# Keys of a pair formed ahead of the leaf products of the pair in front; convolution and token activation run while the matrix is on its way through DRAM

## The chip, the cores and the metric

One core of a Trainium2 chip runs the whole program. TensorE (PE) does matrix products into eight PSUM banks, VectorE (DVE) and ScalarE (ACT) work elementwise, GpSimd (POOL) does copies, differences and indirect transfers, and SyncE (SP) issues most transfers. Each engine runs its instructions in program order and waits on semaphores for the others. The metric is the device time of one execution in microseconds (us).

## The reference

A layer on x of shape (16, 256, 128): a recurrent attention, LayerNorm, a feed-forward part over eight experts, LayerNorm. What matters here is the attention, for 8 heads with keys of 64 and values of 128 elements:

```python
h = _rms(x, w_norm_in)
conv = conv_b + sum((hp[:, j:j + T, :] * conv_w[:, j] for j in range(CK)))   # CK = 4, causal
h = jax.nn.silu(conv)
q, k, v = h @ wq, h @ wk, h @ wv                    # q and k are scaled to unit length per head
sd = h @ w_spike
ab = jax.nn.silu(h @ w_au + b_au) @ w_ad + b_ad     # the low-rank path
bb = h @ w_beta + b_beta
# for each time step t of 256:
mem = DECAY * mem + sd[t]; hard = mem > THR; mem = mem - hard * THR
s = s * alpha[..., None]                            # alpha from ab and the spikes
s = s + beta[..., None] * k[t] (v[t] - k[t] s)      # delta rule, shortened
out[t] = s^T q[t]
...
gate = sigmoid(silu(x @ w_u1 + b_u1) @ w_u2 + b_u2)
y = x + (y @ w_out) * gate
y = y + (silu(h2 @ w_ff1) * (h2 @ w_ff3)) @ w_ff2   # h2 = _rms(y, w_ffn)
```

## The kernel before, in words

The 256 time steps are cut into 8 chunks of 32 (`CH`); a chunk holds 32 steps of all 16 sequences, 512 tokens (`TOK`), and is worked on as a whole. `iterations` writes the body once for the first chunk, once in a hardware loop for chunks 1 to 6, and once for the last. `body(c, nxt, last)` is chunk c's work, into which the front of the next chunk (`nxt`: normalisation, convolution, membranes, decays) and the head of the chunk before (`last`: gate, feed-forward of the attention block, LayerNorm, routing) are woven. The order on each engine is that in which the code is written. A pass has three stages.

1. **The pairs.** The 8 heads go in 4 pairs p (`HP`). On PE `keys(c, p)` forms k and q of a pair from h (L1114, into the banks `read` and `write`). ACT's `keys` copies them to SBUF (L882), ACT's `squares` squares them out of the same banks (L891, into r and w) and so frees the banks; PE's `squares` sums these over the head by a matmul with an indicator (L1128) and so frees r and w for the next pair (`kqsq_used`). ACT's `factors` makes a pair's eight exponentials of decays (L921 to L931) from differences that GpSimd takes. DVE's `leaf_products(c, p)` multiplies keys and exponentials (L1521, L1522); PE's `leaves` forms the products within blocks of 8 steps (L1146). `cross_products` (L1532 to L1547) and PE's `crosses` (L1170, L1171) do the same between blocks; the last of these products is kend, which PE's `turn_ends` transposes (L1238). `turn` and `project` (L1219, L1228) finish the output of the chunk before, and `mean_square` (L1063) is the normalisation's mean for the next chunk. `mask_leaves`, `mask_cross` and `unit_rows_of` put a triangular matrix of 32 by 32 per head and sequence together; `norms` and `scaled_rows` (L1616) scale its rows.
2. **The solve.** SP stores the matrix to DRAM (`a_d`, L658) and loads it back, turned so that a partition holds one matrix (`na`, which lies in kq_blk, L664). DVE inverts it in `solve` by 31 steps j of two instructions (L1643, L1649), the second using the first's result. Between them stand instructions that do not depend on them: `membrane(n)`, 64 instructions (L1440, L1443) that run the next chunk's membranes through its 32 steps, each on the result of the one before, and the head's stages, which the table `stages` puts behind certain j. `pace` lets PE run the head's matmuls and two fillers (L1286) at every fourth j. `convolve(nxt)` (L1398 to L1405) stands in the stage before, at pair 2, behind `unit_rows_of`; `silus(nxt)` (L1416 to L1423) at the end of that stage: it makes h, waits for PE's low-rank matmul and makes au. ACT's `tokens` gives both their tanh. PE's `tokens` (L1071, L1076) forms the low-rank input and the drives sd0 to sd3, and ACT's `drives` copies these to mem (L852); DVE's `driven` waits for them.
3. **The tiles.** With the inverse (`u_d`, loaded to ub) eight tiles of 4 heads are read, predicted and written: r (L1719) is values less prediction; PE L1307, L1322, L1334, L1349; the state is L1729. `decays(nxt, step)` is woven in.

The head begins in the solve: PE multiplies x with wu1 (`u1`, L233), DVE makes zu (L330), ACT its tanh (`tu`, L293), DVE the product (L333); PE `u2`, ACT `gate` (L296), DVE `y1` (L337, L340), then `h2`, four feed-forward stages 0 to 3, and row statistics. Its x comes by a transfer that SP issues as the first thing of its pass, into the buffer that holds the normalisation's factor until the convolution has read it:

```python
            if last:
                sp_e.wait_ge(hn_ready.sem, hn_ready.at(nxt if nxt else c, 1))
                settle(c)
                sp_e.dma_start(xsq[:, :], a["xT"][last.loop + last.plus]).then_inc(hd.x_loaded.sem, 16)
            sp_e.wait_ge(ca_ready.sem, ca_ready.at(c, HP))
```

hn is the first result of `convolve`; ca is what `scaled_rows` writes.

## Time and profile before

| | us |
|---|---|
| median of 3 runs (lowest to highest) | 1876.25 (1864.84 to 1890.15) |
| the profiled execution | 1873.82 |
| its span in the profile | 1871.8 |
| busy: PE, DVE, ACT, POOL | 1449.1, 1274.1, 634.8, 360.1 |

The profile is of one execution. Its timeline lists the instructions of an engine in order of time; times count from the start of the span. Engines are not busy all the time, and no engine is the bound of the whole: which wait ends last has to be read from each stage. A busy PE is partly modelled, since matmuls overlap.

### The profile page before, as it was taken

How to read it: one execution, taken by the hardware profiler on the slowest of the kernel's cores; microseconds unless marked ns; L12 is line 12 of the kernel's file. 1: busy time of each engine (PE TensorE's matmuls, PEld its weight loads, DVE VectorE, ACT ScalarE, POOL GpSimd, SP SyncE). 2: the span in 40 equal slices, each digit the busy share in tenths (PEclk: the TensorE clock that was granted, in tenths of full speed). 3: DMA queues.
4: the chain of work that ended last, by engine and by line, in shares of the span. 5: the costliest groups of instructions: out<-in, count | busy, mean ns of one | idle time of the engine just before them, and what ended most of it. 6: DMA issues, size and time to landing. Idle time of an engine off the chain costs nothing. (4 is left out here: it accounts for less than half of the span.)

```text
span 1871.8 us, 46841 instructions
## 1 busy us (share of the span) xinstructions
PE 1449.1 (77%) x18540; PEld 946.9 (51%) x18568; DVE 1274.1 (68%) x3341; ACT 634.8 (34%) x1342; POOL 360.1 (19%) x515
## 2 busy tenths in 40 slices
PE   1687988797878887787879786888869897974685
PEld 0343664365525653465436562566436663652665
DVE  5568576966787667866796578765695678534564
ACT  4430243223422262134312352124312442222564
POOL 1210141014201320015101420023001420110232
PEclk8568996899689987998789979896699968996898
DMA  8980001010010001000100001000101000102223
GB/s 252 322 254 18 8 8 30 2 23 20 8 23 21 5 20 29 18 8 19 30 13 12 20 8 23 21 5 19 30 11 19 13 14 12 24 26 99 69 70 125
DMA packets 128139, 81.97 MB, mean 44 GB/s; under 512 B 75185, under 2 KB 118513, under 8 KB 127922
## 3 DMA queue, kind: packets, MB, share of 16 engines
q1 hardware_dynamic: 124466, 69.94, 13.6%
q0 software_dynamic: 3456, 8.95, 1.5%
q8 instruction: 159, 2.61, 0.6%
q14 instruction: 58, 0.48, 0.1%
HBM read 27.72 MB, written 51.15 MB: 42 GB/s over the span
## 5 line engine op out<-in xcount | busy, mean ns | idle before, releaser
L789 POOL COPY kx<-kend_t 32x256 f32<-32x256 f32 x256 | 114.3, 447 | 807.3 <-PE ps L1349 787.5
L1286 PE MATMUL ps<-wv,ident 128*128 128x512 f32 x320 | 173.7, 676 | 10.6 <-DVEq L1654 10.5
L1729 DVE SCALAR_TENSOR_TENSOR state<-state,gam,ps 128x128 f32<-128x128 f32 x512 | 137.4, 339 | 49.1 <-PE ps L1349 49.1
L1673 DVE TENSOR_TENSOR nv<-ps,nrm 128x512 f32<-128x512 f32 x64 | 44.2, 691 | 175.9 <-PE ps L1209 175.4
L1349 PE MATMUL ps<-w,kx 128*64 128x128 f32 x2048 | 127.1, 277 | 0.0
L1643 DVE TENSOR_TENSOR nv<-kq,kq_blk 128x31 f32<-128x31 f32 (+15 forms) x248 | 113.7, 458 | 16.7 <-ACT mem L852 10.8
L1349 PEld LDWEIGHTS ps<-w,kx 128*64 128x64 f32 x2048 | 111.7, 138 | 12.9 <-issue 12.9
L1521 DVE TENSOR_TENSOR kq_leaf<-kq,eleaf 128x1024 f32<-128x1024 f32 x32 | 39.9, 1247 | 112.6 <-ACT kq L882 112.4
L1286 PEld LDWEIGHTS ps<-wv,ident 128*128 128x128 f32 x320 | 66.7, 218 | 94.0 <-issue 77.5
L233 PE MATMUL ps<-eleaf,wf 128*128 128x512 f32 x112 | 62.0, 681 | 50.9 <-DVEq L1654 31.8
L999 ACT ACTIVATE w<-ps 128x512 f32<-128x512 f32 x64 | 38.2, 597 | 173.8 <-PE ps L1307 173.8
L1649 DVE TENSOR_TENSOR kq<-kq,nv 128x31 f32<-128x31 f32 (+15 forms) x248 | 91.5, 369 | 1.1
L1334 PE MATMUL ps<-state,kq_start 64*32 64x128 f32 x2048 | 82.9, 277 | 11.1
L1197 PE MATMUL ps<-state,kq_start 64*32 64x128 f32 x2048 | 82.1, 275 | 5.6
L1012 ACT ACTIVATE ysb<-ps 128x512 f32<-128x512 f32 x64 | 38.3, 598 | 141.6 <-PE ps L1334 141.6
L1228 PE MATMUL ps<-yt,wout 128*128 128x128 f32 x512 | 69.9, 293 | 20.0 <-ACT yt L898 20.0
L1307 PEld LDWEIGHTS ps<-r,ub 128*128 128x128 f32 x512 | 65.3, 194 | 36.2 <-issue 32.2
L1307 PE MATMUL ps<-r,ub 128*128 128x128 f32 x512 | 70.4, 281 | 14.2 <-DVE r L1719 11.8
L1170 PEld LDWEIGHTS ps<-kq_pair 64*32 64x32 f32 x2048 | 50.7, 122 | 58.0 <-issue 52.1
L1209 PE MATMUL ps<-wv,hv 128*128 128x512 f32 x128 | 78.3, 698 | 0.6 <-issue 0.2
L1228 PEld LDWEIGHTS ps<-yt,wout 128*128 128x128 f32 x512 | 64.0, 203 | 25.9 <-issue 19.0
L1322 PE MATMUL ps<-w,ab 32*32 32x128 f32 x2048 | 69.7, 273 | 6.0 <-ACT w L999 6.0
(313 smaller groups left out, 3303.9 us busy)
## 6 DMA issues: line engine op xcount, KB each, us to landing
slot_d<-row SPq DMA_DIRECT2D x16, 2064.0 KB, 20.3
xin<-slot_d SPq DMA_DIRECT2D x39, 129.0 KB, 2.1
a_d<-yt SPq DMA_DIRECT2D x8, 512.0 KB, 2.6
kq_blk<-a_d SPq DMA_DIRECT2D x32, 128.0 KB, 2.8
u_d<-kq SPq DMA_DIRECT2D x8, 512.0 KB, 2.6
ub<-u_d SPq DMA_DIRECT2D x128, 32.0 KB, 1.9
wall<-in_w SPq DMA_DIRECT2D x8, 512.0 KB, 7.9
xt<-in_xT POOLq DMA_DIRECT2D x8, 256.0 KB, 3.4
```

Of the source, the lines that this page charges most:

```text
L789: m = pool.tensor_copy(kx[part, :, b4, :], kend_t[part, g, 2 * q:2 * q + 2, :])
L1197: m = pe.matmul(bp.t[CH * b4:CH * b4 + CH, DV * hq:DV * hq + DV], kq_start[rows, hp, 0, CH * b:CH * b + CH], state[rows, hp, b, :], start= ...
L1209: pe.matmul(bv.t[:, :], hv[:, P * g:P * g + P], wv[:, 512 * q:512 * q + 512], start=True, stop=True).then_inc(bv.full.sem, 1)
L1228: m = pe.matmul(bp.t[:, 0:P], wout[:, hh, :], yt[:, hh, :], start=(hh == 0), stop=(hh == H - 1))
L1286: pe.matmul(bw.t[:, :], ident[:, :], wv[:, 0:512], start=True, stop=True)
L1307: m = pe.matmul(bw.t[:, DV * hq:DV * hq + DV], ub[:, g % 2, 4 * q + hq, :], r[:, hq, :], start=True, stop=True)
L1322: m = pe.matmul(by.t[part, cols], ab[part, hp, 1, 2 * g + h2, :], w[part, hq, :], start=(hq == 0), stop=False)
L1334: m = pe.matmul(by.t[CH * b4:CH * b4 + CH, cols], kq_start[rows, hp, 1, CH * b:CH * b + CH], state[rows, hp, b, :], start=False, stop=(hq ...
L1349: m = pe.matmul(bd[b4 % 2].t[DK * h2:DK * h2 + DK, o:o + DV], kx[:, j, b4, DK * h2:DK * h2 + DK], w[:, 2 * j + h2, :], start=True, stop=True)
L1643: dve.tensor_tensor(prod, tu[:, 0:n, j:j + 1].broadcast_to([P, n, m]), na[:, j + 1:CH, j].unsqueeze(1).broadcast_to([P, n, m]), ALU.mult). ...
L1649: i = dve.tensor_tensor(tu[:, 0:n, j + 1:CH], tu[:, 0:n, j + 1:CH], prod, ALU.subtract)
L1729: k = dve.scalar_tensor_tensor(out=state[:, hp, b, :], in0=state[:, hp, b, :], scalar=gam[:, hp, b:b + 1], in1=bd[j].t[:, DV * x:DV * x + ...
```

## The change

Five things are written in another order, and ScalarE gets one small instruction.

- PE: `keys(c, 1)` stands directly behind `keys(c, 0)`; for p from 1 on `keys(c, p + 1)` and `squares(c, p)` stand ahead of `leaves(c, p)`. Before, `leaves` came first, keys behind it and squares behind `crosses`.
- ACT: for pairs 2 and 3 keys, `ends_turned` and squares come first, `factors` behind them; `factors` came first before. `keys(c, 1)` stands ahead of `turned`.
- DVE: `convolve(nxt)` moves out of the pairs to the start of `solve`, behind the last `scaled_rows`; `silus` is split. The token part (h) stands between the head's zu and u1, the low-rank input (zau) behind step j = 0 and its product (au) behind j = 2.
- The membranes start at j = 6; they started at j = 0. The head's stages move to later j.
- ACT: a tanh of one column (`table_probe`) stands ahead of the wait for the convolution, and the low-rank tanh moves behind the head's `tu`.

```diff
@@ ScalarE
         def tokens(f):
 
+            act.activation(table_probe[:, :], eps_t[:, 0:1], ACT.Tanh)
             act.wait_ge(conv_step.sem, conv_step.at(f, 4))
...
             squares(c, 0)
             factors(c, 1)
+            keys(c, 1)
             if last:
                 turned(last, NG - 1)
-            keys(c, 1)
             squares(c, 1)
...
             for p in range(2, HP):
+                keys(c, p)
+                ends_turned(c, p - 2)
+                squares(c, p)
                 factors(c, p)
-                ends_turned(c, p - 2)
                 if nxt:
                     (square_x, rsqrt_x)[p - 2](nxt)
-                keys(c, p)
-                squares(c, p)
...
             if nxt:
+                low_rank(nxt)
                 drives(nxt)
@@ TensorE
             keys(c, 0)
+            keys(c, 1)
+            leaves(c, 0, runs)
             squares(c, 0)
-            leaves(c, 0, runs)
             if last:
                 turn(last, NG - 1)
-            keys(c, 1)
             crosses(c, 0, runs)
             if last:
                 project(last, NG - 1)
-            squares(c, 1)
             turn_ends(c, 0)
             for p in range(1, HP):
-                leaves(c, p, runs)
                 if p + 1 < HP:
                     keys(c, p + 1)
+                squares(c, p)
+                leaves(c, p, runs)
                 crosses(c, p, runs)
-                if p + 1 < HP:
-                    squares(c, p + 1)
                 turn_ends(c, p)
@@ VectorE, solve
-            stages = {0: "y1", 5: "h2", 8: 0, 11: 1, 15: 2, 19: 3, 25: "stat0", 27: "xl", 28: "stat1", 30: "xh"}
-            rest = [n for n in range(2 * CH)] if nxt else []
+            stages = {5: "y1", 10: "h2", 12: 0, 14: 1, 17: 2, 20: 3, 25: "stat0", 27: "xl", 28: "stat1", 30: "xh"}
+            rest = []
             dve.sem_inc(pace.sem, 2)
+            if nxt:
+                convolve(nxt)
             if last:
...
                 head_on_vector(dve, last, room, "zu")
+            if nxt:
+                silu_tokens(nxt)
+            if last:
                 head_on_vector(dve, last, room, "u1")
...
-            if nxt:
-                driven(nxt)
             for j in range(CH - 1):
+                if nxt and j == 1:
+                    low_rank(nxt)
+                if nxt and j == 3:
+                    silu_low_rank(nxt)
+                if nxt and j == 6:
+                    driven(nxt)
+                    rest = [n for n in range(2 * CH)]
...
@@ VectorE, body
                 if p == HP - 2:
-                    if nxt:
-                        convolve(nxt)
                     norms(c)
...
-            if nxt:
-                silus(nxt)
             solve(c, nxt, last)
```

ScalarE in the pairs, from behind the squares of pair 1 (mem to dleaf are the exponentials of pair 2, kend_t the turned ends of pair 0, xsq the square of the next chunk's x, kq the copied keys, r and w the squares). Before:

```order
L921 ACTIVATE mem<-mem 128x512
L922 ACTIVATE eleaf<-dleaf 128x512
L926 ACTIVATE dpair<-dpair 128x32x8
L927 ACTIVATE dpair<-dpair 128x32x8
L926 ACTIVATE dblk<-dblk 128x16x16
L927 ACTIVATE dblk<-dblk 128x16x16
L929 ACTIVATE dend<-dend 128x512
L931 ACTIVATE dleaf<-dleaf 128x512
L940 ACTIVATE kend_t<-ps 128x4x128
L825 ACTIVATE xsq<-xt 128x512
L882 ACTIVATE kq<-ps 128x512 x2
L891 ACTIVATE r<-ps 128x512
```

Now, from the same place:

```order
L887 ACTIVATE kq<-ps 128x512 x2
L945 ACTIVATE kend_t<-ps 128x4x128
L896 ACTIVATE r<-ps 128x512
L896 ACTIVATE w<-ps 128x512
L926 ACTIVATE mem<-mem 128x512
L927 ACTIVATE eleaf<-dleaf 128x512
L931 ACTIVATE dpair<-dpair 128x32x8
L932 ACTIVATE dpair<-dpair 128x32x8
L931 ACTIVATE dblk<-dblk 128x16x16
L932 ACTIVATE dblk<-dblk 128x16x16
L934 ACTIVATE dend<-dend 128x512
L936 ACTIVATE dleaf<-dleaf 128x512
```

The exponentials have moved from ahead of a pair's keys to behind its squares.

TensorE in the pairs, between the cross products of two pairs (headind: sums of squares; ident: turning kend; kq_leaf: leaf products; wk, wq: keys). Before, with the squares of pair 1, the ends of pair 0, the leaves of pair 1 and the keys of pair 2:

```order
L1128 MATMUL ps<-headind,r 128x2 x4
L1128 MATMUL ps<-headind,w 128x2 x4
L1238 MATMUL ps<-ident,kend 128x128 x4
L1146 MATMUL ps<-kq_leaf,km 32x2x32 x32
L1114 MATMUL ps<-h,wk 128x512
L1114 MATMUL ps<-h,wq 128x512
```

Now, with the same pieces:

```order
L1245 MATMUL ps<-ident,kend 128x128 x4
L1121 MATMUL ps<-h,wk 128x512
L1121 MATMUL ps<-h,wq 128x512
L1135 MATMUL ps<-headind,r 128x2 x4
L1135 MATMUL ps<-headind,w 128x2 x4
L1153 MATMUL ps<-kq_leaf,km 32x2x32 x32
```

The keys stand ahead of squares and leaves; the squares, which were first, are behind the keys.

VectorE from the last row scaling to the first membranes, in the hardware loop (yt: scaled rows; kq by L330 and L333: zu and u1 of the head; the copy from kq_blk is the diagonal of the loaded matrix; nv and kq by the solve's two lines; residue and mem: membranes; REGISTER_ALU and ISA rows set up waits). Before:

```order
L1616 TENSOR_TENSOR yt<-ysq,cvec 128x4x64
L1416 SCALAR_TENSOR_TENSOR h<-tz,xt 128x512
L1420 REGISTER_ALU
L1421 TENSOR_SCALAR zau<-ps,bau 64x512
L1423 SCALAR_TENSOR_TENSOR au<-tz,zau 64x512
L1630 REGISTER_ALU
L329 REGISTER_ALU
L330 TENSOR_SCALAR kq<-ps,bu 64x512
L333 SCALAR_TENSOR_TENSOR kq<-kq 64x512
L1633 ISA
L1636 COPY kq<-kq_blk 128x32
```

Now, from the last instruction of the convolution, which follows the row scaling:

```order
L1410 SCALAR_TENSOR_TENSOR xt<-hn,convw,xt 128x512
L1643 REGISTER_ALU
L329 REGISTER_ALU
L330 TENSOR_SCALAR kq<-ps,bu 64x512
L1421 SCALAR_TENSOR_TENSOR h<-tz,xt 128x512
L333 SCALAR_TENSOR_TENSOR kq<-kq 64x512
L1649 ISA
L1652 COPY kq<-kq_blk 128x32
L1664 TENSOR_TENSOR nv<-kq,kq_blk 128x31
L1670 TENSOR_TENSOR kq<-kq,nv 128x31
L1428 REGISTER_ALU
L1429 TENSOR_SCALAR zau<-ps,bau 64x512
```

h stands behind zu; zau, which stood ahead of the diagonal copy, is behind the first solve step. SP's rows have not changed: x for the head, behind hn, stands ahead of the store of the matrix in both.

## Rows read from the trace of the kernel before

**Rows 1.** The page's first line: span and instructions of the profiled execution.

```profile
span 1871.8 us, 46841 instructions
```

**Rows 2.** VectorE's timeline, pairs: start, duration, line, result and inputs, [idle before, releaser].

```profile
673.80 0.68 DVE L1547 TENSOR_TENSOR kend<-kq,dend 128x512 f32<-128x512 f32 x1
...
679.77 1.23 DVE L1521 TENSOR_TENSOR kq_leaf<-kq,eleaf 128x1024 f32<-128x1024 f32 x1 [5.29 <-ACT kq L882]
...
690.52 1.33 DVE L1521 TENSOR_TENSOR kq_leaf<-kq,eleaf 128x1024 f32<-128x1024 f32 x1 [2.25 <-ACT kq L882]
...
700.41 1.23 DVE L1521 TENSOR_TENSOR kq_leaf<-kq,eleaf 128x1024 f32<-128x1024 f32 x1 [1.28 <-ACT kq L882]
```

**Rows 3.** TensorE's timeline: keys of pair 1, projection, squares, the head's first matmul.

```profile
677.04 1.91 PE L1114 MATMUL ps<-h,wq 128*128 128x512 f32 x2
...
680.91 2.02 PE L1228 MATMUL ps<-yt,wout 128*128 128x128 f32 x16
...
702.12 1.03 PE L1128 MATMUL ps<-headind,w 128*128 128x2 f32 x8
...
717.62 1.94 PE L233 MATMUL ps<-xsq,wu 128*64 128x512 f32 x2 [4.46 <-DVE ab L1568]
```

**Rows 4.** ScalarE's timeline: first and last exponential and a square of pair 2, the gate.

```profile
683.15 0.62 ACT L921 ACTIVATE mem<-mem 128x512 f32<-128x512 f32 x1
...
685.93 0.61 ACT L931 ACTIVATE dleaf<-dleaf 128x512 f32<-128x512 f32 x1
...
690.70 0.60 ACT L891 ACTIVATE w<-ps 128x512 f32<-128x512 f32 x1
...
729.72 0.69 ACT L296 ACTIVATE dend<-ps,bu 128x512 f32<-128x512 f32 x1 [1.78 <-PE ps L233]
```

**Rows 5.** Busy time by stretch: length, PE, PEld, DVE, ACT, POOL, granted clock, DMA, GB/s.

```profile
675.00:680.00 5.00, 5.00 (x71) 2.36 (x69) 0.23 (x1) 2.21 (x5) 3.78 (x4) 0.50 0.01 3
...
780.00:785.00 5.00, 3.90 (x13) 1.94 (x15) 3.98 (x7) 0.63 (x1) 0.00 (x0) 1.00 0.34 52
```

**Rows 6.** VectorE's timeline: convolution, last row scaling, diagonal copy.

```profile
709.46 0.75 DVE L1398 SCALAR_TENSOR_TENSOR hn<-xt,wnorm,xsq 128x512 f32<-128x512 f32 x1 [0.49 <-DVE hn L1392]
...
710.83 2.33 DVE L1405 SCALAR_TENSOR_TENSOR xt<-hn,convw,xt 128x512 f32<-128x512 f32 x3
...
718.29 0.42 DVE L1616 TENSOR_TENSOR yt<-ysq,cvec 128x256 f32<-128x256 f32 x1
...
726.24 0.20 DVE L1636 COPY kq<-kq_blk 128x32 f32<-128x32 f32 x1 [0.80 <-DMA kq_blk<-a_d]
```

**Rows 7.** SP's timeline: issue of x for the head and of the matrix's store.

```profile
710.59 0.36 SPq L653 DMA_DIRECT2D xsq<-in_xT  x1
718.88 0.34 SPq L658 DMA_DIRECT2D a_d<-yt  x1
```

**Rows 8.** The page's transfers: queue, count, KB each, median us from issue to landing.

```profile
xsq<-in_xT SPq DMA_DIRECT2D x7, 256.0 KB, 2.6
```

**Rows 9.** VectorE's groups by line from 727.9 to 737.7: count, busy, mean ns, idle before.

```profile
L1649 DVE TENSOR_TENSOR kq<-kq,nv 128x31 f32<-128x31 f32 (+5 forms) x6 | 2.8, 463 | 0.0
L1643 DVE TENSOR_TENSOR nv<-kq,kq_blk 128x31 f32<-128x31 f32 (+5 forms) x6 | 2.1, 351 | 1.5 <-ACT mem L852 1.5
```

**Rows 10.** VectorE's timeline: solve (y1, slowed instruction, h2), the last two membranes, first r.

```profile
730.44 0.69 DVE L337 SCALAR_TENSOR_TENSOR dend<-dend,attn 128x512 f32<-128x512 f32 x1 [1.81 <-ACT dend L296]
...
732.14 1.30 DVE L1649 TENSOR_TENSOR kq<-kq,nv 128x60 f32<-128x60 f32 x1
...
737.76 0.73 DVE L344 SCALAR_TENSOR_TENSOR eleaf<-dend,wffn,dleaf 128x512 f32<-128x512 f32 x1
...
776.99 0.28 DVE L1440 SCALAR_TENSOR_TENSOR residue<-mem 128x64 f32<-128x64 f32 x1
777.30 0.28 DVE L1443 SCALAR_TENSOR_TENSOR mem<-residue,mem 128x64 f32<-128x64 f32 x1
...
783.25 0.68 DVE L1719 TENSOR_TENSOR r<-nv,ps 128x512 f32<-128x512 f32 x1
```

More of the change, by code:

```diff
@@ L478, in attention @@
     eps_t, tiny_t = hd.eps_t, sb("tiny_t", [P, 1])
+    table_probe = sb("table_probe", [P, 1])
     empty = hd.row[:, :, :].rearrange("p g d -> p (g d)")[:, 0:ROW_ID + E * NT32]
@@ L839, in tokens, with low_rank @@
             act.activation(tz[:, :], cacc.rearrange("p b t -> p (b t)"), ACT.Tanh).then_inc(tz_ready.sem, 1)
+        def low_rank(f):
             b = bank_of["au"]
@@ L1034, in first @@
             tokens(c)
+            low_rank(c)
             drives(c)
@@ L1406, in convolve, with silu_tokens @@
                                          in1=cacc, op0=ALU.mult, op1=ALU.add).then_inc(conv_step.sem, 1)
-        def silus(f):
+        def silu_tokens(f):
             dve.wait_ge(tz_ready.sem, tz_ready.at(f, 1))
@@ L1418, in silus, with low_rank @@
                                      op0=ALU.add, op1=ALU.mult).then_inc(h_ready.sem, 1)
+        def low_rank(f):
             b = bank_of["au"]
@@ L1421, in silus, with silu_low_rank @@
             dve.tensor_scalar(zau[:, :], b.t[0:R, :], 0.5, bau[:, 0:1], ALU.mult, ALU.add).then_inc(b.drained.sem, 1)
+        def silu_low_rank(f):
             dve.wait_ge(tau_ready.sem, tau_ready.at(f, 1))
@@ L1775, in first @@
             dve.wait_ge(s_zero, n_made)
-            silus(c)
+            silu_tokens(c)
+            low_rank(c)
+            silu_low_rank(c)
             driven(c)
```

## The prediction

> **What bounds the kernel now.** I take the profiled execution (span 1871.8 us [rows 1], 1873.8 with launch; the median of the three timed runs, 1876.25, is 2.4 above it) and one pass of the loop in it, the fourth of eight, and read VectorE's timeline first. Before the leaf products of pairs 1, 2 and 3 VectorE stands idle 5.3, 2.3 and 1.3 us, each time released by ScalarE's copy of the keys (L882) [rows 2]: 8.8 us in a pass, the most that the first half of the change can give. The reader should also see what the copies waited for: the key matmul of pair 1 took 1.91 us for q alone [rows 3], in a stretch whose granted clock was 0.50, the 1.2 GHz level [rows 5].
>
> The next bound is the round trip of the matrix. The last row scaling (call its end T) is done at 718.29 + 0.42 = 718.71 [rows 6]; the store a_d goes out at 718.88 [rows 7] and VectorE's diagonal copy starts at 726.24 [rows 6], 7.4 us after that issue and 7.5 after T. The convolution lies ahead of T, from 709.46 to 713.16 with a halo copy and a 0.49 us wait in front [rows 6]: 4.3 us on the path. From the diagonal copy to the first residual r (783.25) VectorE is nearly always busy; the idle times are those at L337, 1.81 us for the gate [rows 10], and 1.5 us for the membranes' input at the first solve step [rows 9]. So in this part every instruction put on VectorE costs, and what is taken out ahead of T gains.
>
> **Pair stage, step by step.** The cross products of pair 0 end at 673.80 + 0.68 = 674.5 [rows 2]. With keys and exponentials of pair 1 already made, its leaf products start there and not at 679.77: 5.3 us won. But ScalarE's order is now keys, squares, exponentials, and the squares wait for TensorE to have read the squares of the pair before, which now stand behind the new keys. For pair 2 the line is this. The projection of the last chunk ended at 680.91 + 2.02 = 682.9 [rows 3]; two key matmuls have left the place ahead of it (up to 3.8 us), and as the turning before it still alternates with ScalarE I count 2.0: 680.9. Turning the ends and the copy that frees its bank, about 1.0 (two short pieces, an estimate from copies of 0.6 and less): 681.9. Keys of pair 2, k and q: 3.8 at half clock, 1.9 at full, half of it [rows 3]. Squares of pair 1: two of 1.03, issued 0.9 apart [rows 3]: 1.8. ScalarE's second square 0.6 and the eight exponentials from 683.15 to 685.93 + 0.61, 3.4 in all [rows 4]. Sum: 689.6 at full clock, 691.5 at half, against 690.52 now. So the lead of 5.3 is gone at pair 2. From there to pair 3 the line is: square of x 0.6, its mean on TensorE 1.0 or 1.9, keys 1.9 or 3.8, squares 1.8, ScalarE's square 0.6, exponentials 3.4, and some 0.6 for six hand-overs: 9.9 at full clock, 12.7 at half, against 9.9 now (690.52 to 700.41 [rows 2]). Together pair 3 starts between 0.9 us earlier and 3.8 us later than now; I take the middle, **1.5 later**, because the granted clock of the stage is a mixture today. What follows pair 3 is as before without the convolution: T moves by 1.5 - 4.3 = **-2.8 us**.
>
> **Front of the solve, in times after the new T.** SP still waits for hn (the convolution's first result) to send x for the last chunk's head, and only then issues a_d. hn ends about 1.3 after T (0.15 + 0.49 + 0.75); x went out 0.38 after hn's end at 710.21 and took 0.36 to issue [rows 6, 7], so a_d goes out at 2.05 and not at 0.17: 1.9 us lost, and the diagonal copy starts at 2.05 + 7.36 = 9.4. (The shared queue could add up to the 2.6 us that x takes to land [rows 8], or nothing; I take nothing, since they were issued 0.4 us apart.) x lands at 1.7 + 2.6 = 4.3. The head's first matmul, now hidden, takes 1.94 [rows 3], zu some 0.7 after it: 7.0. The token activation h stands behind zu in VectorE's order, though its tanh is ready at about 5.0: h ends at 7.7 and not at 0.6. What hangs on h then comes late: today, with h directly behind the row scaling (end about 719.3), 11.1 us lie between it and the gate's end (729.72 + 0.69 [rows 4]) through au, the four drives and the prediction of tile 0. ScalarE no longer puts tu between (about 2.0 less), the low-rank input waits for solve step 1 (0.35 more): gate at 7.7 + 11.1 - 1.6 = 17.2.
> VectorE meanwhile: diagonal 0.2, six solve steps without membranes, 2.1 + 2.8 less 1.1 (the 1.30 us instruction, slowed beside GpSimd; its neighbours need 0.2) = 3.8 [rows 9, 10], and zau and au, 1.3, which were hidden in the round trip before. It reaches y1 at 14.7 and waits 2.5 us there, where it waited 1.8 at step 0. After y1's two instructions (1.3) the six steps are done at 18.5. Today that point is 737.76 - 718.71 = 19.05 [rows 10]. So here the change is 0.5 ahead, but twelve membrane instructions are still to do.
> The rest up to the membranes' tail takes 776.99 - 737.76 = 39.2 [rows 10], plus the 1.1 us of the slowed instruction, which now falls into it. The head's stages are closer together (steps 10, 12, 14 for 5, 8, 11): one step less ahead of stage 0, one less ahead of stage 1, where TensorE's results were just in time; that is 0 to 2.0 us of new waits, and I take 1.0. The tail has 14 membranes and not 2, at 777.30 - 776.99 = 0.31 each: 4.3. Then 5.65 to r as now. Sum: 18.5 + 39.2 + 1.1 + 1.0 + 4.3 + 5.65 = 69.8 against 783.25 - 718.71 = 64.5: **+5.3 us** after T (4.3 to 7 by these bounds). The table load that the probe brings forward is hidden in ScalarE's wait and counts nothing: tanh is needed only after the convolution.
>
> **Sum.** A loop pass: -2.8 + 5.3 = +2.5; six of them, +15. The first pass has no head, so no x ahead of a_d and no gate: -2.8 + 3.7 (twelve membranes more in the tail) + 0.5 (waiting for their input) = +1.4. The last has no next chunk: no convolution to win, 1.5 in the pairs and 1.0 for the head: +2.5. Total +19: 1873.8 + 19 = **1893 us**.
>
> **Rivals.**
> *It does what it says* (faster): the exponentials and the gate are never late. Then a pass wins 8.8 and 4.3, loses 1.9 on a_d and 2.7 in the tail (3.7 less the 1.0 that twelve interleaved membranes cost in the steps): -8.5; seven passes -60: 1814. For it: the 8.8 are real idle time. Against it: the line through the squares, longer than the gap it replaces. 12%.
> *TensorE keeps the full clock through the pairs*: pair 3 starts 0.9 earlier, T moves -5.2, the solve costs its lower bound 4.3: -0.9 a pass, about 1867. For it: keys now follow keys without a gap. Against: the same small matmuls in between, in the stage that now has 0.50 to 1.00. 18%.
> *TensorE goes cold ahead of the tiles* (slower). The longer tail keeps TensorE without work some 3.7 us more just before the first tile, where it now runs at granted 1.00 [rows 5]. In the stretch that holds it TensorE is busy 3.90 of 5 us; at half clock that would double, so a cold start costs up to 3.9 us a pass. At 2.5, in seven passes: 1893 + 18 = 1911; from 2.7 a pass on it ends beyond 2%. By the Trainium skill (TensorE: Matmul & The Clock Gate, section "HAM oscillation — how this bites in real kernels") gaps between bursts re-throttle the array and each burst then starts cold; by that rule this rival's 1911 would be the sum, while the row of the first tile, at 1.00 behind today's shorter gap, leaves it at 1893. 25%.
>
> **How the numbers follow.** The forecast, 1893, has 45%, with a range of its own of 1873 to 1915 (0 to 3.8 in the pairs, 4.3 to 7 behind T). The range 1858 to 1922 leaves out the first rival and the upper end of the third. Two per cent, about what a measurement of this kernel can tell from no change, is 37 us: faster only by the first rival, 11%; slower by most of the third and the upper end of the forecast, 22%; within, 67%.
>
> **What would show it.** Right: the leaf products of pair 1 start at once, those of pairs 2 and 3 wait for ScalarE's exponentials and no longer for the keys; a_d is issued right behind x, some 2 us after T; VectorE idles at L337 in solve step 5; fourteen membranes stand alone ahead of the first r. Wrong: no idle time ahead of pairs 2 and 3 (the first rival), a granted clock near 1.00 throughout the pairs (the second), or 0.50 in the first tile (the third). If h is not held up by zu, my gate is about 2.5 us too late.

## The result

The changed kernel takes 1931.3 us (median of four runs, 1930.7 to 1938.4) against 1874.6 for the kernel before it in the same comparison: a ratio of 1.030, with a 95% interval of 1.023 to 1.038. It is slower, by about three times the 19 us that were forecast. Ratios are taken over the fast runs of each kernel, so they differ a little from those of the medians. The profiled execution has a span of 1936.5 us, 64.7 more than that of before; it is the slowest of the four (1938.4), so its rows show some 7 us more than the median does.

The page of the changed kernel (engines: busy time, share of the span, instructions; the last row is TensorE's granted clock in tenths, in 40 slices):

```profile
span 1936.5 us, 46876 instructions
...
PE 1477.5 (76%) x18568; PEld 985.6 (51%) x18568; DVE 1292.8 (67%) x3341; ACT 635.6 (33%) x1350; POOL 381.6 (20%) x515
...
PEclk8568986899678976898688976998688977897898
```

The mean granted clock fell from 0.860 to 0.830. Where the time went is best seen in the six looped passes. The table gives means over them in us, read from VectorE's timeline: L0 is the start of pair 0's leaf products, T the end of the last row scaling, r1 and r8 the first and the eighth residual r of the tiles.

| stretch | before | after | difference | forecast |
|---|---|---|---|---|
| L0 to T (pairs) | 53.0 | 50.0 | -3.0 | -2.8 |
| T to the diagonal copy | 7.4 | 11.1 | +3.7 | +1.9 |
| diagonal copy to the end of the solve | 49.6 | 51.4 | +1.8 | +3.4 for this row and the next |
| end of the solve to r1 | 8.9 | 11.9 | +3.0 | |
| r1 to r8 (tiles) | 70.6 | 73.5 | +2.9 | 0 |
| r8 to the next L0 | 15.6 | 16.6 | +1.0 | 0 |
| pass | 205.1 | 214.4 | +9.3 | +2.5 |

Six passes make 56 us; the first pass is 5.3 longer (1.4 forecast). The last is 4.2 longer up to its r8 and 2.4 up to the end of the span (2.5 forecast).

**The pairs** went as forecast in their order and in the mean. VectorE's timeline of pass 4 after the change, which answers to [rows 2]:

```profile
700.59 1.22 DVE L1532 TENSOR_TENSOR kq_leaf<-kq,eleaf 128x1024 f32<-128x1024 f32 x1
...
717.99 1.23 DVE L1532 TENSOR_TENSOR kq_leaf<-kq,eleaf 128x1024 f32<-128x1024 f32 x1 [4.67 <-ACT dleaf L936]
...
729.71 1.23 DVE L1532 TENSOR_TENSOR kq_leaf<-kq,eleaf 128x1024 f32<-128x1024 f32 x1 [3.23 <-ACT dleaf L936]
```

Pair 1 no longer waits. Pairs 2 and 3 wait for ScalarE's last exponential (dleaf, L936) and no longer for its copy of the keys. Over the whole execution the waits of this line mostly change their name (VectorE's waits, first of before, then of after: total us, times, longest):

```profile
DVE kq_leaf L1521 <- ACT kq L882: 112.4, 31, 8.6
```

```profile
DVE kq_leaf L1532 <- ACT dleaf L936: 57.9, 15, 4.7
...
DVE kq_leaf L1532 <- ACT kq L887: 34.6, 7, 8.6
...
DVE dend L337 <- ACT dend L296: 24.9, 6, 4.5
...
DVE kq_pair L1543 <- PE ps L1178: 22.4, 10, 3.2
```

112.4 us before, 92.5 after; what is won there is lost again in a new wait ahead of the cross products (kq_pair, 22.4). The row of L337 is the gate's wait, the next thing to read.

**The front of the solve** in the same pass, T being 743.32 + 0.42 = 743.74. The rows are picked from the timeline of all engines, in order of time; they answer to [rows 4, 6, 7, 10]:

```profile
745.10 0.36 SPq L654 DMA_DIRECT2D xsq<-in_xT  x1
...
745.74 0.34 SPq L659 DMA_DIRECT2D a_d<-yt  x1
...
748.23 1.94 PE L233 MATMUL ps<-xsq,wu 128*64 128x512 f32 x2 [5.76 <-DMA xsq<-in_xT]
...
749.23 2.35 SPq L665 DMA_DIRECT2D kq_blk<-a_d  x4
...
750.21 0.74 DVE L330 TENSOR_SCALAR kq<-ps,bu 64x512 f32<-64x512 f32 x1 [2.54 <-PE ps L233]
...
750.87 0.67 DVE L1421 SCALAR_TENSOR_TENSOR h<-tz,xt 128x512 f32<-128x512 f32 x1
...
753.52 2.08 PE L1083 MATMUL ps<-h,wsd 128*128 128x512 f32 x2
...
754.84 0.20 DVE L1652 COPY kq<-kq_blk 128x32 f32<-128x32 f32 x1 [2.51 <-DMA kq_blk<-a_d]
...
755.52 0.74 DVE L1429 TENSOR_SCALAR zau<-ps,bau 64x512 f32<-64x512 f32 x1
...
756.42 4.88 PE L1083 MATMUL ps<-h,wsd 128*128 128x512 f32 x6 [0.82 <-DVE zau L1429]
...
763.76 0.69 ACT L296 ACTIVATE dend<-ps,bu 128x512 f32<-128x512 f32 x1 [1.83 <-PE ps L233]
...
764.48 0.69 DVE L337 SCALAR_TENSOR_TENSOR dend<-dend,attn 128x512 f32<-128x512 f32 x1 [4.42 <-ACT dend L296]
```

The store goes out 2.0 us after T, as forecast, but the round trip takes longer. From the store's issue to that of the loads it is 3.49 us, where it was 2.69 before (721.57 - 718.88, the loads at 721.57 and the store in [rows 7]); from the loads to the diagonal copy it is 5.61, where it was 4.67 (726.24 - 721.57). So the copy stands at T + 11.1 and not at T + 9.4. The low-rank input zau stands behind that copy and one solve step, and the matmuls of three of the four drives (L1083) wait for the bank that it drains. The gate comes at T + 20.7 where 17.2 was forecast.

**The tail and the first tile** of pass 4. TensorE's first drive and VectorE's first two residuals:

```profile
815.05 2.05 PE L1093 MATMUL ps<-au,wad 65*128 65x512 f32 x2 [6.06 <-DVE mem L1462]
...
818.26 0.68 DVE L1736 TENSOR_TENSOR r<-nv,ps 128x512 f32<-128x512 f32 x1
...
823.87 0.69 DVE L1736 TENSOR_TENSOR r<-nv,ps 128x512 f32<-128x512 f32 x1 [1.09 <-PE ps L1204]
```

And the same stretch by windows (columns as in [rows 5]: length, PE, PEld, DVE, ACT, POOL busy, granted clock, DMA share, GB/s):

```profile
806.30:809.30 3.00, 2.69 (x7) 0.90 (x6) 2.79 (x12) 0.00 (x0) 0.00 (x0) 1.00 0.42 175
809.30:815.00 5.70, 0.00 (x0) 0.00 (x0) 5.14 (x14) 0.00 (x0) 0.00 (x0) 0.72 0.30 48
815.00:818.30 3.30, 3.25 (x5) 1.46 (x6) 1.49 (x4) 0.63 (x1) 0.00 (x0) 0.50 0.00 0
818.30:822.00 3.70, 3.70 (x10) 2.15 (x9) 2.32 (x5) 0.00 (x0) 0.00 (x0) 0.50 0.00 0
```

TensorE runs at 1.00 until it has nothing to do, stands idle for 6 us while VectorE works off the tail, and starts the first tile at 0.50, the 1.2 GHz level. That is the third rival's sign. The Trainium skill (TensorE: Matmul & The Clock Gate, section "HAM oscillation — how this bites in real kernels") says that gaps between bursts throttle the array again and each burst starts cold; the trace agrees, 1.00 ahead of this gap and 0.50 behind it.

### The profile page after: what moved, and what is told of

It reads as the page before. It is cut to its first block and busy times, and to the rows that moved or that the text cites. A ratio compares the mean times of both kernels' runs of the same rounds, so it can differ in the third digit from the quotient of the medians.

```text
span 1936.5 us, 46876 instructions
## 1 busy us (share of the span) xinstructions
PE 1477.5 (76%) x18568; PEld 985.6 (51%) x18568; DVE 1292.8 (67%) x3341; ACT 635.6 (33%) x1350; POOL 381.6 (20%) x515
## 5 line engine op out<-in xcount | busy, mean ns | idle before, releaser
L790 POOL COPY kx<-kend_t 32x256 f32<-32x256 f32 x256 | 121.2, 473 | 823.6 <-PE ps L1354 807.1
L1291 PE MATMUL ps<-wv,ident 128*128 128x512 f32 x320 | 167.4, 656 | 6.2 <-DVEq L1675 6.2
L1235 PE MATMUL ps<-yt,wout 128*128 128x128 f32 x512 | 91.8, 353 | 20.0 <-ACT yt L903 20.0
L1235 PEld LDWEIGHTS ps<-yt,wout 128*128 128x128 f32 x512 | 84.8, 259 | 26.1 <-issue 19.0
L1339 PE MATMUL ps<-state,kq_start 64*32 64x128 f32 x2048 | 83.8, 279 | 11.3
L1177 PE MATMUL ps<-kq_pair 64*32 64x32 f32 x2048 | 70.4, 233 | 25.8 <-issue 16.2
L1670 DVE TENSOR_TENSOR kq<-kq,nv 128x31 f32<-128x31 f32 (+15 forms) x248 | 86.3, 348 | 2.5
L1093 PE MATMUL ps<-au,wad 65*128 65x512 f32 x64 | 44.6, 786 | 53.6 <-DVE mem L1462 53.6
L1216 PE MATMUL ps<-wv,hv 128*128 128x512 f32 x128 | 83.8, 742 | 0.0
L1177 PEld LDWEIGHTS ps<-kq_pair 64*32 64x32 f32 x2048 | 60.6, 133 | 43.9 <-issue 37.8
```

The lines of the kernel that those rows point to most:

```text
L790: m = pool.tensor_copy(kx[part, :, b4, :], kend_t[part, g, 2 * q:2 * q + 2, :])
L1177: pe.matmul(o1[part, :, u, :, :], kq_pair[rows, 0, t:t + CH], second, start=True, stop=True)
L1216: pe.matmul(bv.t[:, :], hv[:, P * g:P * g + P], wv[:, 512 * q:512 * q + 512], start=True, stop=True).then_inc(bv.full.sem, 1)
L1235: m = pe.matmul(bp.t[:, 0:P], wout[:, hh, :], yt[:, hh, :], start=(hh == 0), stop=(hh == H - 1))
L1291: pe.matmul(bw.t[:, :], ident[:, :], wv[:, 0:512], start=True, stop=True)
L1339: m = pe.matmul(by.t[CH * b4:CH * b4 + CH, cols], kq_start[rows, hp, 1, CH * b:CH * b + CH], state[rows, hp, b, :], start=False, stop=(hq ...
```

## The experiments

The theories: mine as recorded (the gate and the tail, with wrong sizes), the pairs' order as the cause, and TensorE's clock in the tiles (third rival). The table has the kernels' means over the six looped passes, in us as above, and the ratio to the kernel before with its 95% interval. The runs were made on three occasions, each with runs of the kernel before beside them. Its medians there were 1867.6 (pairs_alone to store_first and tail_warm), 1874.9 (zau_first, tail_warm5, tail_in, early_conv) and 1873.5 (all_three, late_membranes, early_conv_warm3, early_conv2), so a difference of some 7 us between medians of two occasions says little; there the ratios are compared.

| kernel | L0 to T | T to y1 (L337) | T to r1 | r1 to r8 | r8 to next | pass | median | ratio |
|---|---|---|---|---|---|---|---|---|
| before | 53.0 | 11.8 | 66.0 | 70.6 | 15.6 | 205.1 | | 1 |
| after | 50.0 | 20.4 | 74.4 | 73.5 | 16.6 | 214.4 | 1931.3 | 1.030 (1.023 to 1.038) |
| pairs_alone | 54.2 | 11.8 | 64.7 | 70.8 | 15.2 | 204.9 | 1872.3 | 1.005 (1.001 to 1.010) |
| solve_alone | 48.1 | 19.9 | 74.3 | 73.0 | 16.9 | 212.3 | 1922.3 | 1.027 (1.019 to 1.035) |
| store_first | 49.9 | 18.5 | 73.3 | 71.4 | 15.9 | 210.4 | 1908.2 | 1.021 (1.013 to 1.029) |
| zau_first | 50.0 | 18.6 | 73.0 | 72.8 | 15.1 | 211.0 | 1916.6 | 1.020 (1.012 to 1.028) |
| all_three | 50.0 | 16.0 | 69.7 | 71.6 | 17.6 | 208.9 | 1908.9 | 1.023 (1.011 to 1.034) |
| tail_warm | 48.4 | 20.6 | 79.5 | 71.6 | 17.7 | 217.2 | 1961.1 | 1.048 (1.039 to 1.056) |
| tail_warm5 | 48.7 | 20.2 | 76.3 | 72.3 | 18.1 | 215.3 | 1941.0 | 1.035 (1.028 to 1.043) |
| tail_in | 50.1 | 19.9 | 74.7 | 72.0 | 15.5 | 212.3 | 1924.3 | 1.027 (1.020 to 1.035) |
| early_conv | 51.2 | 11.3 | 64.6 | 70.8 | 16.0 | 202.6 | 1859.3 | 0.994 (0.990 to 0.997) |
| late_membranes | 51.8 | 11.6 | 64.6 | 71.5 | 16.6 | 204.5 | 1880.1 | 1.007 (1.002 to 1.011) |
| early_conv_warm3 | 51.3 | 11.6 | 64.9 | 71.9 | 17.7 | 205.7 | 1872.5 | 1.002 (0.998 to 1.006) |
| early_conv2 | 50.5 | 12.4 | 66.5 | 70.8 | 15.4 | 203.3 | 1867.6 | 1.006 (0.998 to 1.013) |

### Which half costs: the pairs alone, the solve alone

Edit of pairs_alone, on the kernel before (TensorE; ScalarE's lines likewise in the new order):

```diff
             keys(c, 0)
-            squares(c, 0)
+            keys(c, 1)
             leaves(c, 0, runs)
+            squares(c, 0)
```

> The kernel before with the new order of TensorE and ScalarE in the pairs only; convolution, activation, membranes and the head's stages stay where they were. My forecast as recorded: pair 3 starts 1.5 us later a pass and nothing behind it changes, so T (end of the last row scaling) moves by +1.5 in eight passes, +12 us, about 1886. Read from the two traces instead (leaf products of pair 0 to those of pair 3: 34.7 us a pass before, 35.9 after, means of the six looped passes): +1.3 a pass, about +10, 1884. A rival puts the loss of the whole change here, since TensorE's new order also starts the next pass: then this kernel comes out above 1900, with a granted clock below that of before (0.86).

Measured: 1872.3 us, 1.005 times the kernel before. From pair 0 to pair 3 the leaf products take 35.9 us a pass and not 34.7, +1.2 where +1.5 was forecast; from T on nothing is later. The pairs are not the cause.

solve_alone is the changed kernel with those lines put back.

> The changed kernel with the pairs' order of before: convolution and activation in the round trip, membranes from step 6, the head's new stages. My forecast as recorded: -4.3 us at T and +5.3 behind it, +1 a pass, 1880 to 1883. From the traces: behind T the passes are longer by 3.6 us to the diagonal copy, 1.8 in the solve, 3.0 to the first r, 2.9 in the tiles and 1.0 to the next pass, 12.3 in all, less the 4.3 of the convolution: +8 a pass, +55, 1925 to 1932. The rival that blames the pairs' order for the tiles and the end of a pass: about 1900 here, and the tiles as long as before (70.6).

Measured: 1922.3 us. Tiles 73.0 and not 70.6: they are slow without the new pairs' order, so it is not that order which makes them slow. By the ratios the solve part alone makes 2.7 of the 3.0 per cent.

### What makes the gate late: the store, the low-rank input, and h

Edit of store_first, on the changed kernel (SP):

```diff
-            if last:
-                sp_e.wait_ge(hn_ready.sem, hn_ready.at(nxt if nxt else c, 1))
-                ... (x's load)
             sp_e.wait_ge(ca_ready.sem, ca_ready.at(c, HP))
             ...
             sp_e.dma_start(a_d..., ca)
+            if last:
+                ... (the same wait and load)
```

> The changed kernel with SP issuing the matrix's store ahead of x (which still waits for the convolution's first result). Store theory: x's 256 KB and its wait hold up the matrix by 3.6 us a pass; now the store goes out 0.2 after T and the diagonal copy starts 7.5 to 9 after T and not 11.1, and all behind it is earlier by 2 to 3.5: -14 to -25 us, 1906 to 1917. Gate theory: the first steps of the solve end at the gate's wait (L337) in any case, which hangs on x, zu and h; the diagonal copy is earlier but the wait at L337 grows by the same: 0 to -1 a pass, 1924 to 1931, and x lands later by up to 2 us, which could make it +1 a pass.

Measured: 1908.2 us, 23 less than the changed kernel (by the ratios 0.9%, with intervals that overlap). The timeline of pass 4 (T at 735.66), SP's issues, VectorE's diagonal copy and its first instruction behind the gate:

```profile
735.95 0.33 SPq L655 DMA_DIRECT2D a_d<-yt  x1
...
736.91 0.36 SPq L659 DMA_DIRECT2D xsq<-in_xT  x1
...
738.75 2.31 SPq L665 DMA_DIRECT2D kq_blk<-a_d  x4
...
744.37 0.20 DVE L1652 COPY kq<-kq_blk 128x32 f32<-128x32 f32 x1 [0.33 <-DMA kq_blk<-a_d]
...
754.08 0.69 DVE L337 SCALAR_TENSOR_TENSOR dend<-dend,attn 128x512 f32<-128x512 f32 x1 [4.20 <-ACT dend L296]
```

From store to loads it is 2.80 us again, and the diagonal copy stands 8.7 after T. The way from the loads to that copy stays at 5.62. The store theory holds in total, yet the gate theory names the way: the gate itself came 1.9 us earlier, since zau stands behind the diagonal copy. I had expected it not to move. Of the 4.0 us a pass, 1.1 are won up to r1 and 2.1 in the tiles; the latter are the clock's drops in later tiles, which none of its six passes has (see the clock below); whether that is the edit's doing is not shown.

Edit of zau_first, on the changed kernel (VectorE):

```diff
+            if nxt:
+                low_rank(nxt)
             dve.wait_ge(na_loaded.sem, na_loaded.at(c, 64))
 ...
-                if nxt and j == 1:
-                    low_rank(nxt)
```

> The changed kernel with the low-rank input (L1429) ahead of the diagonal copy and not behind solve step 0, so that the drives' matmuls do not wait for a bank that it drains. Gate theory: TensorE's wait of 0.8 us in the drives goes and the four drives, the prediction and the gate come 1 to 1.7 earlier, y1 at 18.8 to 19.4 after T and not 20.4; 0.74 us of VectorE's work moves into its wait for the matrix: -1 to -2 a pass, 1917 to 1925. If the drives are bound by TensorE's half clock alone: 0 to -0.7, 1926 to 1932.

Measured: 1916.6 us, y1 18.6 after T: as the gate theory said. The drives run through (TensorE's timeline): the four drives (each matmul of this shape is counted twice in the rows) in 5.77 us, where they took 7.78 with the wait between them (753.52 to 756.42 + 4.88).

```profile
748.62 5.77 PE L1083 MATMUL ps<-h,wsd 128*128 128x512 f32 x8
```

all_three has both edits, and h ahead of zu:

```diff
                 convolve(nxt)
+                silu_tokens(nxt)
             if last:
                 ...
                 head_on_vector(dve, last, room, "zu")
-            if nxt:
-                silu_tokens(nxt)
```

> The changed kernel with the store issued ahead of x, the low-rank input ahead of the diagonal copy, and the token activation h ahead of zu. Gate theory: singly, the first two moved y1 by 1.9 and 1.8 us a pass (they overlap, since the low-rank input stood behind the late matrix), and h ahead of zu lets its first matmul follow the head's at once, 1.5 earlier; y1 at 16.5 to 17.5 after T, first r at 71 to 72 and not 74.4, the tiles 71.5 to 72.5: -4 to -5 a pass, 1895 to 1905, still slower than before, since the convolution's 4.3 us on VectorE now stand where other work used to fill the round trip, and the 14 membranes in the tail stay. Rival: with the three waits gone the convolution's gain shows: below 1885.

Measured: y1 16.0 after T and r1 69.7 after T. The forecast had 69.8 for the changed kernel itself. That the two agree is luck: the forecast's sum holds a store behind x, h behind zu and zau behind a solve step, and this kernel has none of the three. VectorE's timeline, T at 737.27: h ends at T + 5.3 and not 7.8, and the wait at L337 is 2.35 and not 4.42.

```profile
741.89 0.69 DVE L1421 SCALAR_TENSOR_TENSOR h<-tz,xt 128x512 f32<-128x512 f32 x1 [0.69 <-ACT tz L841]
...
753.34 0.69 DVE L337 SCALAR_TENSOR_TENSOR dend<-dend,attn 128x512 f32<-128x512 f32 x1 [2.35 <-ACT dend L296]
```

The time, 1908.9, missed the 1895 to 1905 expected. The looped passes did what was expected up to r8, but r8 to the next pass took 17.6, and the first pass 195.4 us (191.6 in the changed kernel). It is still slower than before, and no faster than store_first: what the last two edits won up to r1 (3.6 a pass) was lost again, most of it at the ends of the passes (1.7 a pass) and in the first pass (7.8). That place stays open.

### The clock in the first tile

tail_warm, on the changed kernel (TensorE, behind the last pace), with ten fillers, and tail_warm5 with five:

```diff
+            for k in range(10):
+                pe.matmul(bw.t[:, :], ident[:, :], wv[:, 0:512], start=True, stop=True)
             if nxt:
                 decays(nxt, 0)
```

> The changed kernel with ten more filler matmuls on TensorE (the kind it already runs at each pace) behind the last pace, ahead of the first drive of the tiles: they fill the 6 us in which TensorE has nothing to do while VectorE works off the membranes' tail. The result is unchanged. Cold theory (third rival): the first tile then runs at a granted clock of 1.00, from the first to the eighth r it is 70.5 us and not 73.5, and the first drives take 1.0 and not 2.05: -3 to -4 us a pass, -21 to -28, 1903 to 1911. If the tail's 4.3 us of membranes are all that counts: 1928 to 1935, the same within 4 us.

> As the run with ten fillers, with five: one filler took 0.875 us there (8.75 for ten, in two passes each), so ten ended 3 us after VectorE wanted the first drive; five take 4.4 and end in time. Cold theory: first drives at 1.0 and not 2.05 us, first r 0.5 to 1 earlier, first to eighth r 70.6 to 71.6 (71.6 with ten fillers) and not 73.5: -2.5 to -4 a pass, 1903 to 1914. If the clock is not what costs: 1927 to 1936.

Measured: 1961.1, slower, and 1941.0, which the ratios do not tell from the changed kernel. With ten, the fillers ended after VectorE wanted the first drive (8.75 us for them in pass 4). Five fitted in pass 4, whose rows are these (TensorE's fillers and first drive, then VectorE's first two residuals):

```profile
814.83 4.45 PE L1293 MATMUL ps<-wv,ident 128*128 128x512 f32 x10
...
819.12 1.02 PE L1093 MATMUL ps<-au,wad 65*128 65x512 f32 x2
...
823.43 0.68 DVE L1738 TENSOR_TENSOR r<-nv,ps 128x512 f32<-128x512 f32 x1
...
826.95 0.69 DVE L1738 TENSOR_TENSOR r<-nv,ps 128x512 f32<-128x512 f32 x1 [0.40 <-PE ps L1204]
```

The window of that first tile (columns as above):

```profile
819.20:823.40 4.20, 3.12 (x8) 1.13 (x8) 2.33 (x5) 0.63 (x1) 0.00 (x0) 1.00 0.01 3
```

At a granted clock of 1.00 the first drive takes 1.02 and not 2.05 us, and the second residual follows the first after 3.52 us and not 5.61. So 2.1 us is the price of the cold first tile in that stretch of pass 4, the dearest of the six; in the mean the changed kernel's second residual follows the first after 4.5 us, 1.0 more than before. As a remedy the fillers failed: in four of the six passes r1 came 14.7 to 14.9 us after the end of the solve and not 12.0.

The other 1.9 of the 2.9 us that the tiles lost lie in later tiles. Between the sixth and the seventh residual five of the six passes of the changed kernel take 17.8 to 18.0 us, where five of before take 16.4; between the fourth and the fifth, three take 11.6 to 11.7 and not 10.0. VectorE's wait in the former place and the window between those two residuals, pass 4 of after, then of before:

```profile
874.11 0.69 DVE L1694 TENSOR_TENSOR nv<-ps,nrm 128x512 f32<-128x512 f32 x1 [8.67 <-PE ps L1216]
```

```profile
864.76:882.75 17.99, 14.69 (x198) 11.09 (x192) 9.25 (x20) 5.61 (x10) 3.29 (x6) 0.91 0.00 1
```

```profile
835.35 0.69 DVE L1673 TENSOR_TENSOR nv<-ps,nrm 128x512 f32<-128x512 f32 x1 [7.03 <-PE ps L1209]
```

```profile
827.63:843.99 16.36, 13.06 (x198) 9.58 (x192) 9.26 (x21) 5.62 (x10) 3.30 (x6) 1.00 0.01 3
```

The granted clock falls there too, to a mean of 0.91. All six passes with five fillers have this second drop (18.0), though five of them start their first drive at 1.00; none of store_first has it, though none starts at 1.00. So it is a cost beside the cold start and not part of it, and it is what kept the tiles slow where the first tile was warm. What decides whether a pass has it is not shown.

tail_in, on the changed kernel (VectorE):

```diff
+                if rest and j >= CH - 15:
+                    membrane(rest.pop(0))
                 if j % 4 == 0:
                     dve.sem_inc(pace.sem, 1)
```

> The changed kernel with a third membrane instruction in each of the last 14 solve steps, so that none is left for the tail. VectorE does the same work in the same number of instructions. Cold theory: TensorE's stretch without work ahead of the first drive is as short as before the change (7.4 us from the end of the solve to the first r, not 11.9), the first tile runs at 1.00: first r 1 earlier, tiles 70.6, together -3 to -4 a pass, 1903 to 1911. Work theory (only VectorE's instructions count): the end of the solve moves by 4.3 and the tail goes, first r where it was, tiles 73.5: 1927 to 1936.

Measured: 1924.3 us. The end of the solve moved by 3.9, the stretch behind it shrank by 3.4, and r1 stayed where it was (74.7 after T): the work theory, as far as r1. The tiles took 72.0 and not 73.5, so the clock is worth some of the rest, about half of what the cold theory asked. In single passes it is either 7.0 us to r1 and 73.1 in the tiles, or 9.7 to 10.0 and 70.3 to 72.0: the cold stretch falls on one side of r1 or on the other. The 73.1 and the 72.0 hold the later drop, too.

### Where the convolution costs nothing

early_conv is the kernel before with the pairs' new order and the convolution between pair 1's unit rows and pair 3's leaf products, where pairs_alone waits 3.5 us:

```diff
+                if nxt and p == HP - 3:
+                    convolve(nxt)
                 if p == HP - 2:
-                    if nxt:
-                        convolve(nxt)
                     norms(c)
```

(x's square, its mean and its root move ahead on ScalarE and TensorE.)

> Not the changed kernel: the kernel before with the pairs' new order, and the convolution put where VectorE waits for pair 3's exponentials (behind the unit rows of pair 1), x's square and its mean ahead of that. The token activation, the membranes and the head's stages stay as before. If a transfer's cover is what the convolution lost (my reading now): its 4.3 us then go into an idle time of 3.5 ahead of pair 3, T is 3 to 3.5 earlier a pass against the pairs alone, nothing behind T moves: 1872 less 21 to 25, 1847 to 1852. Rival: x's mean on TensorE and ScalarE's square of x, now ahead of pair 2, delay its keys and the exponentials by 1 to 2.5 us (2.5 with the mean at half clock): 1855 to 1868.

Measured: 1859.3 us, 0.994 times the kernel before: faster than both, though by only 0.6% of the kernel before, with an interval just clear of 1. T is 3.1 us a pass earlier than in pairs_alone, as expected, and the gate is where it was before the change. Over pairs_alone the median gained 13 us; by the ratios, each to its own occasion, it is 1.1%, some 21 us, the lower end of the 21 to 25 expected. The pass is 2.3 shorter, not 3.1, and the first pass 4.3. VectorE's timeline, where pair 3 now follows the convolution without a wait:

```profile
703.75 2.33 DVE L1405 SCALAR_TENSOR_TENSOR xt<-hn,convw,xt 128x512 f32<-128x512 f32 x3
705.99 1.22 DVE L1521 TENSOR_TENSOR kq_leaf<-kq,eleaf 128x1024 f32<-128x1024 f32 x1
```

late_membranes is early_conv with the change's table and membranes:

```diff
-            stages = {0: "y1", 5: "h2", 8: 0, 11: 1, 15: 2, 19: 3, ...
-            rest = [n for n in range(2 * CH)] if nxt else []
+            stages = {5: "y1", 10: "h2", 12: 0, 14: 1, 17: 2, 20: 3, ...
+            rest = []
 ...
+                if nxt and j == 6:
+                    driven(nxt)
+                    rest = [n for n in range(2 * CH)]
```

> The kernel with the convolution ahead of pair 3, and on top of it only the change's later membranes (from solve step 6) and head stages (5, 10, 12, ...), without the convolution in the round trip. It prices the two halves of the solve part apart. If the tail and the cold start behind it make the loss: 12 membranes more in the tail, +3.7, less 1.0 in the first steps, and a cold first tile, +2 to +3: +5 to +6 a pass, 1894 to 1900. If the loss comes from the convolution's place and the gate that it makes late: +0 to +2.7 a pass, 1859 to 1877.

Measured: 1880.1 us, some 20 above early_conv (by the ratios 1.3%): 3 us above the second range and far below the first. In the profiled executions r1 comes 64.6 after T in both kernels. The tail of 14 membranes is there (11.2 us from the end of the solve to r1 against 8.1), but the solve is 3.0 shorter, so up to r1 it costs nothing there. The pass is 1.9 longer, 0.6 of it in the tiles and 0.6 ahead of T, which is some 11 us in six passes; the profiled execution, 1870.3, is the second fastest of ten, so the rest of the 20 is in no row. So the late membranes and stages do cost, about a third of the change's loss if the prices add up; the larger part, by difference, goes with the convolution's place and the late gate behind it.

Two attempts at more:

```diff
-KEEP_WARM = 2
+KEEP_WARM = 3
```

> The kernel with the convolution ahead of pair 3, with three filler matmuls at each pace and not two. Before the change three of six looped passes come to the first r 3 us later (10.4 and not 7.4 from the end of the solve) with a granted clock of 0.5 to 0.75 ahead of it. Cold theory: more fillers keep the clock up and those passes go: -3 us in one to three passes, 1850 to 1857. Rival: 0.875 us more of TensorE's time at each pace delays the head's matmuls between them, whose stages VectorE waits for: +0.5 to +1 a pass, 1862 to 1867.

Measured: 1872.5 us, with a higher granted clock (0.871 against 0.858) and a pass 3.2 us longer, in the tiles and at the end of the pass. Neither account had that place. The 1.1 in the tiles is the later drop of the clock again: all six passes take 17.8 to 18.0 us between the sixth and the seventh residual, one of early_conv does. The end of the pass stays open.

early_conv2 leaves x's square and mean where they were and moves ScalarE's two steps for the root only:

```diff
-                    (square_x, rsqrt_x)[p - 2](nxt)
+                if nxt and p == 2:
+                    square_x(nxt)
+                    rsqrt_x(nxt)
```

> As the kernel with the convolution ahead of pair 3, but x's square and mean stay behind pair 2's exponentials, where they were, and only the two steps that make its root (L830, L832) come ahead of pair 3's keys on ScalarE, which wait for TensorE there. If x's mean and square, put ahead of pair 2, cost the 1.0 us by which the leaf products of pair 2 came later (24.9 us after those of pair 0, not 23.8): pair 2 is back at 23.8 and T 1.0 earlier: 1850 to 1856. Rival: the root waits for the mean and holds up pair 3's keys by 1 to 2 us: 1860 to 1870.

Measured: 1867.6 us. Pair 2 starts 24.2 us after pair 0, not 24.9, and T is 0.6 earlier, but r1 is 1.9 later after T. Its interval (0.998 to 1.013) does not say whether it gains; inconclusive.

## Why the prediction was wrong

The direction was right, the likeliest class (within 2%) and the range were not. By its own steps:

**The pairs, right in the mechanism; the size in part by luck.** +1.5 at pair 3 was forecast, +1.2 measured as a mean, and T came 3.0 earlier, 2.8 forecast. But in pass 4, from which the forecast was worked out, pair 3 came 3.1 later and T only 1.2 earlier; the means agree because pass 7 of before is long (57.2 us from L0 to T, the others 51.5 to 53.3). The line through keys, squares and exponentials is the one that the waits show.

**The store's issue, right; its transfer, wrong.** The forecast took nothing for the shared queue, "since they were issued 0.4 us apart". It was 0.64 apart, and the store and the loads behind it took 1.7 us longer (T + 11.1, not 9.4). Of that, 0.8 lies between the store and the loads, behind x on the same queue, and goes when the store is ahead of x. The Trainium skill (SBUF — State Buffer, section "Can I just issue two DMAs to hit both halves?") says that two transfers at once serialize; the trace leans that way, 3.49 us from the store to the loads against 2.69, and store_first at 2.80 with x behind the store. The other 0.9 lies in the loads themselves (5.61 against 4.67), is there in store_first too (5.62), and in the first pass, which sends no x (5.3 against 4.7). It goes with the solve part (5.5 in solve_alone, 4.5 in pairs_alone, same pass); what makes it is not shown.

**The gate, the step that failed.** It was forecast at T + 17.2 and came at T + 20.7: from h's end to the gate's end the sum had 9.5 us, and it was 764.45 - 751.54 = 12.9. Two terms were mis-sized. The low-rank input was counted at 0.35 for standing behind solve step 0; it stood behind a diagonal copy that was itself late, and came 2.0 us later after h than before (3.98 against 721.28 - 719.32 = 1.96): 1.65 too little. And the 2.0 credited for ScalarE's tu was won and lost again. TensorE's wait of 2.09 for ScalarE ahead of the last two drives is gone, but a term that the sum put at nothing took its place, the clock: the drives now fall into a stretch with a granted clock of 0.55, where three of them, a count of six, take 4.88 us, 0.81 a count; before, the last two, a count of four, took 1.96, 0.49 a count, at 1.00. That is 1.9 us more for the three. TensorE's timeline of before, then the windows of before and of after over the drives:

```profile
725.35 1.96 PE L1076 MATMUL ps<-h,wsd 128*128 128x512 f32 x4 [2.09 <-ACT mem L852]
```

```profile
721.10:727.40 6.30, 4.21 (x17) 1.44 (x20) 2.97 (x5) 2.88 (x6) 0.00 (x0) 1.00 0.53 83
```

```profile
753.50:761.30 7.80, 6.98 (x13) 2.33 (x16) 4.86 (x15) 2.30 (x4) 0.00 (x0) 0.55 0.00 0
```

So the six steps were done at T + 22.2 and not 18.5: 3.7 of the 4.7 us by which r1 missed its forecast (74.5 in pass 4, 69.8 forecast). all_three bears out that the late gate holds r1: without the three waits the instruction behind the gate's wait starts 4.4 us earlier a pass (T + 16.0) and r1 comes 4.7 us earlier.

**The rest of the solve and the tail, right.** From the end of y1's second instruction to r1 the sum was 51.3; measured 818.26 - 765.89 = 52.4. The reading of the tail as a loss up to r1 was not borne out where no gate holds the first steps up: in the rows of late_membranes, membranes moved out of them are repaid there.

**The third rival came true beside the forecast, in part.** I set it up as another case; it is an addition. Its sign, 0.50 in the first tile, is in the rows. The tiles took 73.5 and not 70.6, within its bound of 3.9 a pass, but only 1.0 of the 2.9 lies in the cold first tile; the rest is the clock's drop in later tiles, of which the rival did not speak. A sum of forecast and rival would have said 1911; with the gate's 3.7 a pass, 1933. That this lands near 1931 is a sum made afterwards and partly luck.

**The baseline was too good.** Pass 4 of before is one of three looped passes with r1 7.4 us after the solve; the next three have 10.3 to 10.6. There the last two fillers took 3.41 us, where they take 1.96 in pass 4. In the mean of before r1 comes 66.0 after T and not 64.5, so against means the forecast of this part missed by 3.1 a pass (8.4 and not 5.3) and not by 4.7. TensorE's timeline of before, pass 5:

```profile
980.88 3.41 PE L1286 MATMUL ps<-wv,ident 128*128 128x512 f32 x4
984.13 1.02 PE L1086 MATMUL ps<-au,wad 65*128 65x512 f32 x2
```

**The first pass.** I gave it 1.4 us; it lost 5.3. Its store now goes out earlier, at 126.8 us, into the long fill of another buffer (slot_d) on the same queue, and its loads follow after 6.7 us (133.50 - 126.83), where they followed after 2.6. SP's timeline, before, then after, and the window of after ahead of the store:

```profile
132.29 0.34 SPq L658 DMA_DIRECT2D a_d<-yt  x1
134.90 2.36 SPq L664 DMA_DIRECT2D kq_blk<-a_d  x4
```

```profile
126.83 0.34 SPq L659 DMA_DIRECT2D a_d<-yt  x1
133.50 2.41 SPq L665 DMA_DIRECT2D kq_blk<-a_d  x4
```

```profile
122.00:126.80 4.80, 3.35 (x48) 1.71 (x37) 4.59 (x13) 2.08 (x3) 1.67 (x4) 0.61 0.99 299
```

That is not what lost the 5.3, though: T came 6.6 us earlier there, counted from L0, and the diagonal copy still 1.9 earlier. The loss lies behind it: 2.2 in the solve, 3.9 from its end to r1 and 4.4 at the end of the pass, less 3.2 in the tiles. Of these the forecast had the tail; the end of this pass takes 13.7 us or 18.1 in every kernel here (store_first 13.7, early_conv 18.1), and why is open.

**The other rivals.** "It does what it says" fell with the waits on the exponentials. "Full clock through the pairs" fell too: the granted clock from L0 to T of pass 4 is 0.66 (0.69 before).

**Still open.** What decides whether the granted clock drops in the later tiles of a pass, what makes the loads of the matrix 0.9 us longer, and what makes the end of a pass swing between 15 and 22 us. The gate and the clock in the tiles are shown as places of the loss; how the 57 us divide among gate, late membranes and clock rests on kernels whose medians scatter by several us.

## What to carry to other kernels

A wait of one engine (here VectorE's, for a transfer) may be the cover of others: before work is moved into it, list what ran there on all engines and where it goes, since its chain (here x, zu, h, drives, gate) is late by all that is put ahead of it. Look for an idle time whose neighbours wait for nothing of yours: the same convolution gained when it was put where VectorE waited for ScalarE, if only 0.6% of the whole. And a rival that costs on its own place is added to the forecast, not weighed against it.

## What was not expected of the hardware

Fillers that are meant to keep TensorE's clock up become a delay once it is down: two that took 1.96 us at a granted 1.00 in pass 4 of before took 3.41 at 0.56 in pass 5, and r1 came 3 us later. A kernel that starts its tiles at 1.00 can still lose the clock inside them: 18.0 us between the sixth and the seventh residual at a mean of 0.91, 16.4 at 1.00. A store of 512 KB issued 0.64 us behind a load of 256 KB on the same queue reached its waiter 0.8 us later than alone (3.49 against 2.69), and one issued into a running fill 4.1 us later (6.7 against 2.6).
